# A masked two-level graph attention network on one core: layer 2 by pairs of tiles, its denominators by eights

## The reference, cut to what matters

```
e      = leaky_relu(u_i + v_j)              # slope 0.2
e      = where(adj[i, j] > 0, e, -9e15)
att    = softmax(e, axis=1)
h      = elu(att @ features)                # layer 0 adds x and normalises its rows
```

## Time and profile before

| | |
|---|---|
| time, median of 3 runs | 3555.91 us (3555.37 to 3556.21) |
| the profiled execution | 3555.84 us, its span 3554.1 us |
| PE busy | 3220.6 us, 91% |
| DVE busy | 2877.7 us, 81% |
| ACT busy | 2261.3 us, 64% |
| mean granted PE clock | 0.983 |
| layer 2, first mask to last denominator | 2389.05 to 3533.71 us of the span |

### The profile page before, as it was taken

How to read it: one execution, slowest core, us unless ns; L and a number is a source line. 1 busy time by engine, 2 the same in 40 slices (tenths; PEclk the granted TensorE clock), 3 DMA queues, 4 the chain that set the end, 5 groups by cost and what they waited for, 6 DMA issues and landing times. The chain is left out here.

```text
span 3554.1 us, 60890 instructions
## 1 busy us (share of the span) xinstructions
PE 3220.6 (91%) x24158; PEld 1141.0 (32%) x24269; DVE 2877.7 (81%) x5283; ACT 2261.3 (64%) x3933; POOL 116.3 (3%) x138
## 2 busy tenths in 40 slices
PE   1579999999999997899999999979999999999998
PEld 0323333333333332333333333333333333333332
DVE  5468888888888875799999999976887888778876
ACT  0346666767766675577777877745656665666555
POOL 0000000000000000000000000000000000000000
PEclk9989999999999998999999999979999999999999
DMA  8999999999999941122212121211121112111200
GB/s 255 281 347 344 343 336 337 336 338 338 343 336 332 338 153 49 66 85 86 98 72 98 72 109 71 97 69 51 56 84 67 71 56 84 67 71 56 84 32 7
DMA packets 414127, 578.88 MB, mean 163 GB/s; under 512 B 294402, under 2 KB 315010, under 8 KB 389266
## 3 DMA queue, kind: packets, MB, share of 16 engines
q1 hardware_dynamic: 409458, 564.40, 49.4%
q0 software_dynamic: 4384, 10.59, 0.9%
HBM read 430.10 MB, written 77.69 MB: 143 GB/s over the span
## 5 line engine op out<-in xcount | busy, mean ns | idle before, releaser
L562 ACT ACTIVATE prob<-eps,v2col 128x512 f32<-128x512 f32 x3072 | 1945.5, 689 | 904.2 <-PE eps L736 894.8
L1126 DVE SCALAR_TENSOR_TENSOR eps<-ua,v8col,cb 128x512 f32<-128x512 f32 x2800 | 1975.6, 756 | 405.4 <-ACT prob L562 398.0
L780 PE MATMUL acc<-prob,feat 128*64 128x512 f32 x6144 | 1531.8, 605 | 6.7 <-ACT acc_s L570 6.7
L736 PE MATMUL eps<-nt,nbig 128*32 128x512 fp8e4 (+2 forms) x7852 | 964.6, 383 | 152.8 <-DVE eps L1126 136.3
L736 PEld LDWEIGHTS eps<-nt,nbig 128*32 128x32 bf16 (+2 forms) x7852 | 337.8, 100 | 866.9 <-DVE eps L1126 538.0
L780 PEld LDWEIGHTS acc<-prob,feat 128*64 128x64 f32 x6144 | 384.0, 136 | 596.1 <-issue 365.3
L789 PE MATMUL den<-prob,ones 128*32 128x512 f32 x4096 | 546.0, 605 | 0.0
L965 DVE TENSOR_SCALAR mi<-stage 128x1024 uint8<-128x1024 int32 x512 | 353.5, 692 | 66.3 <-DMA stage<-in_adj_dram 66.0
L974 DVE TENSOR_SCALAR edges<-nt 128x2048 int32<-128x2048 int32 x192 | 235.0, 1224 | 32.2 <-PE misc L747 16.8
L747 PE MATMUL misc<-edges,oneh 128*32 128x512 fp8e4 x3072 | 191.6, 392 | 70.6 <-DVE edges L974 55.8
L789 PEld LDWEIGHTS den<-prob,ones 128*32 128x32 f32 x4096 | 80.6, 108 | 417.7 <-issue 417.7
(11 more groups left out here) (153 smaller groups left out, 1229.9 us busy)
## 6 DMA issues: line engine op xcount, KB each, us to landing
stage<-in_adj_dram SPq DMA_DIRECT2D x512, 512.0 KB, 6.6
nt<-nt_d SPq DMA_DIRECT2D x128, 1024.0 KB, 5.2
nt_d<-nt SPq DMA_DIRECT2D x64, 1024.0 KB, 7.2
ub<-u_d SPq DMA_DIRECT2D x48, 256.0 KB, 5.1
xy_d<-xin POOLq DMA_DIRECT2D x32, 256.0 KB, 3.2
xin<-xy_d SPq DMA_DIRECT2D x32, 256.0 KB, 2.9
nt<-mi SPq DMA_TRANSPOSE x256, 7.3
xin<-in_x_dram SPq DMA_DIRECT2D x16, 128.0 KB, 6.3
```

The source lines that it names most:

```text
L562: nc.scalar.activation(prob[:, j % TS, :], eps[:, j % ES, :], ACT.Exp, bias=v2col[:, j:j + 1]).then_inc(s_p, 1)
L736: mm = nc.tensor.matmul(et[c:c + cols, :], nbig[:, c:c + cols], edge, start=False, stop=True, skip_group_check=True, tile_position=(0, c))
L780: mm = nc.tensor.matmul(acc[h:h + C, :], feat[:, l % 2, j, 0:C], prob[:, j % TS, :], start=(k == 0), stop=(k == NT // 2 - 1))
L1126: dv.scalar_tensor_tensor(eps[:, j % ES, :], ua[:, par, :], v8col[:, j:j + 1], cb[:, par, :], ALU.add, ALU.max).then_inc(s_fill, 1)
```

## The change

In layer 2 the groups become pairs (`GROUP`) with a lag of 2, and the masks go in halves of 64 columns. Only line 780 stands in the group, and it alone counts in `s_main`. The denominators leave the group: when t mod 8 is 3, the two quads of the eight tiles before are done together, 16 matmul records in two rounds of four strips, and count in a new semaphore `s_den`. Tiles stay needed for longer, so layer 2 has sixteen slots of probabilities: the eight of `prob` and eight in `mi`. Layers 0 and 1 keep their order; ACT's waits for slots, `acc` and `den` are rewritten to match.

```diff
-GROUP = (QUAD, 2, QUAD)
-LAG = (1, 2, 1)
+GROUP = (QUAD, 2, 2)
+LAG = (1, 2, 2)
+DEN = 2 * QUAD
+DLAG = 3
 TS = 2 * QUAD
+SLOTS = (TS, TS, 2 * TS)
-MASK_COLS = (32, 64, 32)
+MASK_COLS = (32, 64, 64)
...
+        more = mi[:, :, :].rearrange("p s w -> p (s w)").bitcast(F32).rearrange("p (s w) -> p s w", w=BI)
+        s_den = sem("probs_in_denominators")
+        def weights(l, j):
+            n = j % SLOTS[l]
+            return prob[:, n, :] if n < TS else more[:, n - TS, :]
...
             def probs(l, b, j):
-                if j % GROUP[l] == 0 and not (l == 0 and b == 0 and j < TS):
+                if l < 2 and j % GROUP[l] == 0 and not (l == 0 and b == 0 and j < TS):
                     act.wait_ge(s_main, summed(l, b, j - TS + GROUP[l] - 1))
+                if l == 2 and j % DEN == 0:
+                    if b == 0 and j < TS:
+                        act.wait_ge(s_main, group(2, 0, 0))
+                    elif b or j >= 2 * TS:
+                        act.wait_ge(s_den, b * (NT // DEN) + j // DEN - 1)
                 act.wait_ge(s_z, tile(l, b, j) + 1)
-                nc.scalar.activation(prob[:, j % TS, :], eps[:, j % ES, :], ACT.Exp,
+                nc.scalar.activation(weights(l, j), eps[:, j % ES, :], ACT.Exp,
...
             def denominators_out(l, b):
-                act.wait_ge(s_main, group(l, b, NT // GROUP[l]))
+                if l:
+                    act.wait_ge(s_den, (b + 1) * (NT // DEN))
+                else:
+                    act.wait_ge(s_main, group(l, b, NT // GROUP[l]))
...
             def sums(l, b, k):
-                if l == 1:
+                if l:
                     main(l, b, k).then_inc(s_main, 1)
                 else:
                     main(l, b, 2 * k)
                     main(l, b, 2 * k + 1).then_inc(s_pair, 1)
-                    denominators(l, b, k)
+                    denominators(l, b, k).then_inc(s_main, 1)
+            def two_quads(b, g):
+                denominators(2, b, 2 * g)
+                denominators(2, b, 2 * g + 1).then_inc(s_den, 1)
...
+                        if l == 2 and t % DEN == DLAG:
+                            g = t // DEN - 1
+                            if g >= 0:
+                                two_quads(b, g)
+                            elif tail:
+                                two_quads(b - 1, NT // DEN + g)
                         if tail:
                             tail_step(l, b - 1, t)
...
+                if l == 2:
+                    two_quads(NB - 1, NT // DEN - 1)
```

More of the change, by code:

```diff
@@ L557, in probs @@
             def probs(l, b, j):
-                if j % GROUP[l] == 0 and not (l == 0 and b == 0 and j < TS):
+                if l < 2 and j % GROUP[l] == 0 and not (l == 0 and b == 0 and j < TS):
                     act.wait_ge(s_main, summed(l, b, j - TS + GROUP[l] - 1))
+                if l == 2 and j % DEN == 0:
[3 more added lines that the diff above has]
+                        act.wait_ge(s_den, b * (NT // DEN) + j // DEN - 1)
                 act.wait_ge(s_z, tile(l, b, j) + 1)
-                nc.scalar.activation(prob[:, j % TS, :], eps[:, j % ES, :], ACT.Exp,
+                nc.scalar.activation(weights(l, j), eps[:, j % ES, :], ACT.Exp,
                                      bias=v2col[:, j:j + 1]).then_inc(s_p, 1)
             def sums_out(l, b, par):
-                if l == 1:
+                if l:
                     act.wait_ge(s_main, group(l, b, NT // GROUP[l]))
                 else:
-                    act.wait_ge(s_pair, (den_blocks(l, b) + 1) * (NT // QUAD))
+                    act.wait_ge(s_pair, (b + 1) * (NT // QUAD))
                 nc.scalar.activation(acc_s[:, :], acc[:, :], ACT.Copy).then_inc(s_acce, 1)
             def denominators_out(l, b):
-                act.wait_ge(s_main, group(l, b, NT // GROUP[l]))
+                if l:
+                    act.wait_ge(s_den, (b + 1) * (NT // DEN))
+                else:
+                    act.wait_ge(s_main, group(l, b, NT // GROUP[l]))
                 nc.scalar.activation(den_s[:, :], den[:, :], ACT.Copy).then_inc(s_dene, 1)
@@ L779, in main @@
                         pe.wait_ge(s_acce, blk(l, b))
-                    mm = nc.tensor.matmul(acc[h:h + C, :], feat[:, l % 2, j, 0:C], prob[:, j % TS, :],
+                    mm = nc.tensor.matmul(acc[h:h + C, :], feat[:, l % 2, j, 0:C], weights(l, j),
                                           start=(k == 0), stop=(k == NT // 2 - 1))
@@ L788, in denominators @@
                 for i in range(QUAD):
-                    mm = nc.tensor.matmul(den[32 * i:32 * i + 32, :], ones[:, 0:32], prob[:, (QUAD * k + i) % TS, :],
+                    mm = nc.tensor.matmul(den[32 * i:32 * i + 32, :], ones[:, 0:32], weights(l, QUAD * k + i),
                                           start=(k == 0), stop=(k == NT // QUAD - 1))
-                mm.then_inc(s_main, 1)
+                return mm
             def sums(l, b, k):
-                if l == 1:
+                if l:
                     main(l, b, k).then_inc(s_main, 1)
```

## The result

| | before | after |
|---|---|---|
| median | 3556.06 us (3555.37 to 3556.68, 4 runs) | 3498.07 us (3495.49 to 3499.27, 4 runs) |
| the profiled execution | 3555.84 us, span 3554.1 | 3499.27 us, span 3497.5 |
| a block of layer 2 | 71.01 us | 67.38 us |
| a block of layer 1 | 56.87 us | 56.87 us |

The ratio is 0.9836, with a 95% interval of 0.9819 to 0.9853: 58 us less. A second comparison gave 0.984 (0.9827 to 0.9854), 3498.37 us.

The account below looks back on a forecast made before the run. PE bounds layer 2, the only layer changed (967.48 of 994.17 us busy); DVE bounds layer 1. 3555.84 - 36 (width) + 15.5 (full-width steps) - 32 (stalls) = 3503.3, so 3503 us; range 3489 to 3535.

Parts of the forecast that it names:

- plain stretch, changes of width: Layer 2's eights without other steps: half as many width changes there and back, 128 at 0.28 us, 36 us less.
- full-width steps: Layer 2 pairs around full-width matmuls pay more for width changes: 1.0 us more in 14 blocks, 15.5 us altogether.
- stalls: PE's waits in a layer 2 block, at head, maxima's rows and edges: 0.44 for 2.56 us, 32 us less over 15 blocks.
- The head's 1.86: PE's wait for masks of tiles 52 to 55 while DVE works on the maxima; denominators at 51 shrink it to 0.06 us.
- the wait for the maxima's row: PE's 0.58 us wait in the head goes, as rows are spread 1.3 us later, longer than ACT's 0.60 copy.
- Hidden costs at nothing: In layer 2, copying `acc` and the new semaphore waits cost nothing; reading `mi` nothing, within 13 us either way.
- Stalls that stay: Rival at layer 2's head: its chain moves with PE and waits return at 56 to 59 or edges; 3535; 20% with fills that bind in the pairs.
- fills that bind in the pairs: Rival in layer 2: DVE's fills add 0.2 to 0.3 us an eight, 32 us back; 3535; 20% with Stalls that stay.
- The slower one: Rival in layer 2: the burst of denominators starves other engines, 8.2 us an eight, 73 us a block, 3587 us; 5%.
- More than forecast: Rival in layer 2: no stall at edges, full-width pairs at 0.20, 0.4 + 0.3 us a block less, 3492 us; 8%.
- That width doesn't cost by itself: Rival in layer 2: the first fp32 matmul after a width change costs that anyway; -32 and +15.5 stay, 3540 us; 7%.
- One price of 0.14: Same price for every width change in layer 2, full width too: 37 a block before, 29 after, 18 us saved.

Follow-up runs that it names:

- Pairs with strips: The changed kernel with layer 2's masks in strips of 32 columns again, pairs and denominators by eights kept: 71.95 us a block, 3571.26 us, ratio 1.0049.
- halves alone: The kernel before with only layer 2's masks put in halves of 64 columns, groups of four kept: 70.60 us a block, 3549.87 us, ratio 0.9984.
- the groups of four: The changed kernel with groups of four and a lag of one again in layer 2, denominators by eights: 70.11 us a block, 3539.79 us, ratio 0.996.

## Why the prediction was right, point by point

Predicted 3503 us, 53 less; measured 3498.07, 58 less. Block by block:

| term | predicted, a block | measured |
|---|---|---|
| plain stretch, changes of width | -2.24 (8 x 0.28) | -2.55 (8 x 0.32) |
| full-width steps | +0.9 to 1.0 | +1.0 |
| stalls | -2.1 (2.56 to 0.44) | -2.1 (2.52 to 0.41) |
| block | 71.0 to 67.6 | 71.01 to 67.38 |

- **The bound** was right: PE in layer 2, and layer 1 unmoved at 56.87.
- **Plain stretch.** The mechanism was right, one size was off. I took 0.28 us as the price of going to strips and back, wherever it stands. It is that in the old order, with 0.05 of it the lengthening of sums that follow directly on a change. In the new order masks stand there and lengthen by only 0.02, and a there and back is 0.24. So an eight went from 7.454 to 7.135, 0.32 less and not 0.28: 5 us over 128 eights. (The written sum 4 x 1.29 + 2 x 0.86 + 0.28 gives 7.16, not 7.18; the 7.18 has 2.59 for four tiles.) Pairs with strips and halves alone show both parts.
- **Full-width steps** came out as worked out. The pair at t = 8 shows the price of 0.24: 0.10 on the sums before it, 0.09 on its masks, 0.05 on its sums (0.91 where 0.86 is plain). The measured 1.0 for the block is what is left of 3.64 beside the other two terms, not read off rows.
- **Stalls.** The head's 1.86 fell to 0.05 (0.06 by hand), the edges went from 0.12 to 0.36 (0.38 by hand), and the wait for the maxima's row went. That one was 0.52 and not 0.58: the mask of 58 came 0.97 after that of 57 (2892.39 and 2893.36), and in that idle stretch lies the spreading matmul that the trace of before has no record of (0.23 in after). That the denominators' place does it is shown by moving them: 1.5 us come back. That pairs are needed beside it is shown by the groups of four, where the 0.58 and the waits at the edges return.
- **Hidden costs at nothing:** the copies of `acc` and `den`, ACT's wait on `s_den` and sums over `mi` show no wait of PE. Two tiles later the copy of `acc` costs 0.65, so the cover named for it was the right one.
- **The edges of the layer:** 14 blocks save 50.9 us, about 2.5 more than predicted: 4.4 more in the plain stretch, less 1.7 because the sum took the lower 0.9 for full-width steps. The first and the last save 3.7 together, as predicted, but by luck of the split: 2.7 and 1.0 where the sum had 1.9 and 1.8. The spans differ by 56.6; 0.8 of the rest lies in layer 2's start, where the same 64 counting matmuls met another clock, and 1.1 before layer 1's first turn step (1510.53 and 1509.43), which the change doesn't touch. So of the 4 to 5 us by which the forecast was too slow, about 2 lie outside the change. The clock (1.00 is 2.4 GHz, 0.50 is 1.2) is the third value from the right in the second part of the counting, before and after; in both PE had been idle for 7.4 us before the counting. That began at 2373.25 and 2372.08; the clock rose within the stretch in before and was up for all of it in after:

```profile
2376.20:2380.40 4.20, 3.57 (x40) 1.15 (x32) 1.55 (x2) 0.58 (x1) 0.00 (x0) 0.65 1.00 421
```

```profile
2375.00:2378.50 3.50, 2.48 (x40) 0.67 (x32) 1.58 (x2) 0.60 (x1) 0.00 (x0) 1.00 1.02 424
```

- **The rivals.** Stalls that stay and fills that bind in the pairs would have shown as idle PE; there is 0.17 us of it in a block. The slower one needs DVE idle in the denominators; even four banks don't bring it about. "More than forecast" was the nearest rival in time (3492), but by another cause than named there: the edges' wait stayed. That width doesn't cost by itself is refuted by pairs with strips.
- **The Trainium skill** (TensorEngine Tiling (Array Packing), Key Properties) says of every change of tiling mode that it drains TensorE, and makes no difference between them. One price of 0.14 gave 18 us for all changes of width together. The terms measured are 16 x 2.55 less 16 x 1.0, about 25 us (the first and last block taken like the others). The direction holds; the rows add that the price depends on the neighbours.

## What to carry to other kernels

When one engine is full, look at its start-to-start distances, not its busy time: here 0.28 us in each 3.73 was neither work nor idle, and came from the neighbours' tile widths. Give neighbours one width and collect the odd one out in few long runs; then place such a run, which needs nothing fresh, right where another engine has its longest chain. Check that place by working each producer's due times through one period, with all its side jobs in their order, for they decide more than the plain rate.

## What the runs showed that was not expected

- A change of column width on TensorE has two parts here: about 0.1 us at the change (0.10 from halves to strips, 0.11 from strips to halves) and 0.05 us in fp32 sums directly behind it (1.86 or 1.87 against 1.81 for four tiles, 0.91 against 0.86 for two), 0.02 in masks.
- Half as many mask matmuls of twice the width take the same time: 0.43 us for two tiles in halves, 0.54 in strips, if the 0.11 measured for a change is taken off.
- One scores' bank less costs 2.7 us of 67.4 in a block that PE bounds, and 3.8 of 56.9 in one that DVE bounds, though plain eights change by only 0.08 us.
